# Expert outputs scattered to a row per token and rank, and two chunks' steps five tiles earlier

## The chip, the cores and the metric

The kernel runs on one core of a Trainium2 chip. The metric is the device time of one execution in microseconds. TensorE multiplies, VectorE, ScalarE and GpSimd work on rows in SBUF, SyncE (SP) issues most transfers, and GpSimd issues those whose row numbers are in a table (indirect transfers).

## The reference

The input is 2 x 1024 tokens of 128 numbers, T = 2048 rows. Two layers follow one another; each normalises its input and adds two branches to it.

```
xn = layernorm(x)
x  = x + [xn + attention(layernorm(xn))] + experts64(xn)
xn = layernorm(x)
x  = x + wkv_mix(xn) + experts8(xn)
```

Attention has 16 heads of 8 numbers, and queries and keys of unit length. `experts64` sends each token to its 3 best of 64 experts (rank 0, 1, 2). An expert takes the first 64 rows sent to it, later ones are dropped, and it computes `gelu(rows @ w1 + b1) @ w2 + b2`; a token's result is the sum of its three expert rows, each times its gate. `wkv_mix` is a recurrence over the tokens of a sequence (running maxima and two weighted sums), with a gate and an output product. `experts8` computes all 8 experts for all tokens and keeps the two best by their gates.

## The kernel before

The tokens are worked in 16 tiles of 128 rows, four tiles to a chunk, so there are four chunks of 512. Every engine has its own instruction stream, written out by hand in program order, and the engines meet only at semaphores (`wait_ge`). No scheduler moves anything: where a step stands in the code of an engine is where it runs.

The attention is the backbone. It is a loop over 128 tiles (16 groups of a chunk and four heads, 8 key tiles each): TensorE makes the scores of a tile (line 1347), ScalarE takes their exponential (line 564), TensorE multiplies by the values (line 1361). All else of the first half is put between tiles: `if n == 98: combine(0)` in VectorE's stream means that VectorE does that step when it comes to tile 98. TensorE and ScalarE have tables of the same kind.

From tile 32 to tile 79 the 64 experts run in 8 rounds of 6 tiles; a round does four pairs of experts. GpSimd gathers the rows of the pairs from `xn_rows` in DRAM with the list `IDX` (line 388), TensorE and VectorE compute, and at the end of a round VectorE writes the round's 4 x 128 output rows to `Y` (line 924, `moe_y`). SP stores `Y` to `slot_out`, a DRAM table by expert and place (lines 315 and 318). After the last round, at tile 83, GpSimd gathers each chunk's rows back, 12 indirect transfers of 128 rows for a chunk (line 397), three at a time, since each set of three waits for the one before. `YGS` holds two chunks, so chunks 2 and 3 are gathered when 0 and 1 have been used.

VectorE adds chunks 0 and 1 to `BASE` (`combine`, line 933), GpSimd chunks 2 and 3 (lines 406 and 410: a product over 1536 columns and three sums over 512). Then the second layer follows for each chunk: attention's output product, `x1_norm` (lines 945 to 954, which for chunks 2 and 3 waits for GpSimd's sums), `x1_scale` (975), transposes on TensorE (`normed`, 1473), key, value and gate products, and the recurrence: `time_mix` (1037, 1039), `time_mix_states` (1051, 1053), `time_mix_out` (1058 to 1064), `time_mix_end` (1067, 1070). GpSimd does four products of each chunk's recurrence (`mix`, 417 to 424). `finish` on TensorE (1512, 1515) closes the chunk.

Behind the attention, from about 381 us, comes the tail: 32 steps, one for each chunk and expert of `experts8` (`up2` line 1609, `down2` line 1618, `accumulate` on VectorE, line 1078), with the recurrence of chunk y put at the steps MIX_FROM[y] = 1, 11, 21 and after: VectorE does `time_mix` of chunk 1 at step 3, `time_mix_states` at step 5, `x1_norm` of chunk 2 at step 6, `time_mix_out` of chunk 1 at step 7, `x1_scale` of chunk 2 at step 8, `time_mix_end` of chunk 1 at step 9.

How the slots are found: VectorE numbers each token's place within its expert (`slots`), makes one-hot rows of places (`RANK`) and of experts times token number (`WHO`, `slot_hots`), TensorE multiplies them (`invert`, line 1440), and VectorE copies the product as `IDX` (`slot_tokens`).

Of the kernel before, what the change touches and what calls it, by code (L numbers as in the profile page):

```python
# [7 lines left out]
ALU = mybir.AluOpType  # L8
ACT = mybir.ActivationFunctionType
AX = mybir.AxisListType.X  # L10
F32 = mybir.dt.float32
# [5 lines left out]
P = 128  # L17
# [6 lines left out]
def build(nc, x_d, ln_w_d, ln_b_d, qkv_w_d, qkv_b_d, out_w_d, out_b_d, gate_w_d, gate_b_d, w1_d, b1_d, w2_d, b2_d,  # L24
# [53 lines left out]
    MIXED = (94, 109, 111, 112, 120, 125)  # L78
# [5 lines left out]
    slot_out = nc.dram_tensor("slot_out", [SLOTS, D], F32, kind="Internal").ap()  # L84

    with ExitStack() as ctx:
# [24 lines left out]
        WHO = carve(RA, 6144, 1536, F16).rearrange("p (k t e) -> p k t e", k=TOPK, e=E0)  # L111
# [65 lines left out]
        SLF = sb("slot_f", [P, TOPK, NT])  # L177
        SLG = sb("slot_gather", [P, TOPK, NT], U32)
        TOK = sb("token", [P, NT])
        IDX = sb("slot_token", [P, NPAIR], U32)  # L180
        MH = sb("mask_bf", [P, NT, E0], BF16)
# [43 lines left out]
        for i in range(4):  # L225
# [9 lines left out]
            ranked inverted slot_ready b1_in b1_ps b1_sb b2_in bt_ps bt_sb up_done h_sb gelu_done htr_ps htr_sb down_done y_sb  # L235
# [25 lines left out]
        def _(sp):  # L261
# [15 lines left out]
            sp.dma_start(WG[:], wg_d).then_inc(s["l1_in"], 16)  # L277
            sp.dma_start(MB2[:], mb2_d).then_inc(s["l1_in"], 16)
# [26 lines left out]
            for G in range(ROUNDS):  # L305
# [12 lines left out]
            sp.dma_start(slot_out[P * RING * (ROUNDS - 1):P * RING * ROUNDS].rearrange("(i p) d -> p i d", p=P), Y).then_inc(s["y_out"], 16)  # L318
# [12 lines left out]
        def _(pool):  # L331
# [4 lines left out]
                            pattern=[[-1, P]], channel_multiplier=1).then_inc(s["const_ready"], 1)  # L336
            link(g.memset(VA, 0.0))
# [8 lines left out]
                            pattern=[[1, P]], channel_multiplier=-1)  # L346
            g.iota(iota_e[:], [[1, E0]], base=0, channel_multiplier=0, allow_small_or_imprecise_dtypes=True)
# [37 lines left out]
            for m in range(NPAIR):  # L385
                if m >= RING and m % RING == 0:
                    pool.wait_ge(s["h_sb"], m)
                g.indirect_dma_start(ring_in[m % RING], None, xn_rows, bass.IndirectOffsetOnAxis(IDX[:, m:m + 1], 0),  # L388
                                     bounds_check=T - 1, oob_is_err=True).then_inc(ring_in_x[m % RING], 16)
            pool.wait_ge(s["y_out"], 16 * ROUNDS)  # L390

            def gather(c):
                for t in range(CH * c, CH * c + CH):
                    if t > CH * c:
                        pool.wait_ge(gathered[c], 16 * TOPK * (t - CH * c))
                    for k in range(TOPK):
                        g.indirect_dma_start(YGS[c % 2][:, t - CH * c, k, :], None, slot_out, bass.IndirectOffsetOnAxis(SLG[:, k, t:t + 1], 0),  # L397
                                             bounds_check=SLOTS - 1, oob_is_err=True).then_inc(gathered[c], 16)

            def combine(c):  # L400

                pool.wait_ge(gathered[c], 16 * TOPK * CH)
# [23 lines left out]
            gather(0)  # L426
            pool.wait_ge(gathered[0], 16 * TOPK * CH)
# [1244 lines left out]
```

## Time and profile before

| | us |
|---|---|
| three runs, median (lowest to highest) | 523.83 (523.05 to 525.02) |
| span of the profiled execution | 525.1 |
| the profiled execution's own time, beside its span | not given apart from the span; the highest run is 525.02 |
| TensorE matmul busy | 494.3 (94%) |
| ScalarE busy | 375.1 (71%) |
| VectorE busy | 303.1 (58%) |
| GpSimd busy | 144.1 (27%) |

The busy share of TensorE is high in every stretch, so the shares alone say little: what is to be read is where an engine waits, and for whom. In the rows, a time in brackets is the idle time of the engine just before the instruction, and behind the arrow stands what ended it. PE is TensorE (PEld its weight loads), DVE VectorE, ACT ScalarE, POOL GpSimd.

### The profile page before, as it was taken

To read this page: it belongs to the slowest core of one execution; us is meant where nothing else is said; L and a number is where in the kernel's file an instruction comes from. 1 tells how busy PE (TensorE), PEld (TensorE's weight loads), DVE (VectorE), ACT (ScalarE), POOL (GpSimd) and SP (SyncE) were. 2 spreads that over 40 slices of the span, in tenths; PEclk is the share of its full clock that TensorE was granted. 3 is DMA by queue.
4 is the path that set the end of the run, shared out by engine and by line. 5 is a ranking of instruction groups with operands and counts; after the bars stand their busy time and mean duration, and the time that the engine had idled before them with its cause. 6 is when DMAs were issued, how large, how long until landed. Compare 5 with 4: busy or idle time off the path is not lost.

```text
span 525.1 us, 11527 instructions
## 1 busy us (share of the span) xinstructions
PE 494.3 (94%) x4696; PEld 270.8 (52%) x4696; DVE 303.1 (58%) x790; ACT 375.1 (71%) x464; POOL 144.1 (27%) x133
## 2 busy tenths in 40 slices
PE   6977999999999999999998999999899999999996
PEld 5874223443455455445444232333467766767775
DVE  6799899434343343343330126367937983994895
ACT  3967988786978878978888989888535625553641
POOL 4078000303203203203000445425550755400120
PEclk8997999999999999999998999999899999999999
DMA  5200000565487877977362511100100110000000
GB/s 148 82 1 1 2 1 2 157 216 181 163 238 243 282 243 218 313 238 233 126 201 60 152 32 31 32 1 21 37 6 0 35 38 11 22 0 1 21 1 20
DMA packets 38542, 50.01 MB, mean 95 GB/s; under 512 B 3581, under 2 KB 20250, under 8 KB 38490
## 3 DMA queue, kind: packets, MB, share of 16 engines
q1 hardware_dynamic: 35524, 43.84, 25.4%
q0 software_dynamic: 2560, 5.25, 5.1%
q8 instruction: 37, 0.61, 0.5%
q10 hardware_dynamic: 406, 0.20, 0.1%
q14 instruction: 15, 0.12, 0.1%
HBM read 45.07 MB, written 4.19 MB: 94 GB/s over the span
## 4 chain that ended last, share of the span: by engine, by line
PE 50%; ACT 17%; DVE 6%; issue 5%; DVEq 0%
ACT region_b L564 11%; PE bank L1361 11%; PE scores L1609 9%; PE bank L1618 9%; PE scores L1347 5%; PE bank L1407 4%; PE bank L1395 3%; ACT xn L570 2%; PE bank L1417 2%; PE bank L1478 2%; DVE region_a L1067 2%; ACT L564 2%; ACT L570 2%; DVE base L1078 1%; PE bank L1372 1%
## 5 line engine op out<-in xcount | busy, mean ns | idle before, releaser
L564 ACT ACTIVATE region_b<-scores 128x1024 f32<-128x1024 f32 x256 | 242.4, 1045 | 51.8 <-PE scores L1347 51.6
L1361 PE MATMUL bank<-region_b 128*16 128x256 f32 x2048 | 149.0, 391 | 0.0
L1347 PE MATMUL scores<-region_b 32*128 32x512 f16 x512 | 83.0, 389 | 14.2 <-ACT region_b L564 14.0
L626 ACT ACTIVATE region_b<-scores,small_cols 128x512 f32<-128x512 f32 x64 | 43.6, 685 | 50.3 <-PE scores L1609 50.3
L388 POOL DMA_INDIRECT region_a<-xn_rows,slot_token x32 | 32.5, 1016 | 160.8 <-DVE h_rows L908 108.0
L1361 PEld LDWEIGHTS bank<-region_b 128*16 128x16 f32 x2048 | 42.0, 96 | 57.9 <-issue 42.6
L1618 PEld LDWEIGHTS bank<-region_a,region_b 128*128 128x128 f32 x512 | 62.2, 192 | 15.5 <-issue 15.3
L1347 PEld LDWEIGHTS scores<-region_b 32*128 32x128 f16 x512 | 20.8, 91 | 92.4 <-ACT region_b L564 68.9
L1618 PE MATMUL bank<-region_a,region_b 128*128 128x128 f32 x512 | 62.5, 275 | 0.0
L1609 PE MATMUL scores<-x_rows,region_a 128*128 128x512 f32 x128 | 62.3, 610 | 0.0
L1078 DVE SCALAR_TENSOR_TENSOR base<-bank,g,base 128x128 f32<-128x128 f32 x128 | 36.0, 344 | 28.0 <-PE bank L1618 27.6
L397 POOL DMA_INDIRECT xn<-slot_out,slot_gather x24 | 24.7, 1029 | 65.4 <-DMA slot_out<-slots_io 44.4
L908 DVE COPY h_rows<-bank 128x512 f32<-128x512 f32 x32 | 22.1, 692 | 24.6 <-PE bank L1395 24.6
L924 DVE TENSOR_TENSOR slots_io<-bank,region_a 128x512 f32<-128x512 f32 x8 | 5.5, 692 | 51.4 <-PE bank L1417 51.4
L1395 PE MATMUL bank<-region_a,slots_io 128*64 128x512 f32 x128 | 32.8, 609 | 0.2
L1609 PEld LDWEIGHTS scores<-x_rows,region_a 128*128 128x128 f32 x128 | 22.8, 195 | 19.5 <-issue 19.4
L1417 PE MATMUL bank<-region_a,xn 128*64 128x128 f32 x512 | 32.4, 280 | 0.5 <-issue 0.5
L1417 PEld LDWEIGHTS bank<-region_a,xn 128*64 128x64 f32 x512 | 28.4, 139 | 7.8 <-issue 6.8
L397 POOL DMA_INDIRECT y_rows<-slot_out,slot_gather x24 | 25.5, 1060 | 22.1 <-DMA y_rows<-slot_out,slot_gather 14.2
L916 DVE TENSOR_TENSOR xn<-bank,region_a 128x512 f32<-128x512 f32 x32 | 21.3, 687 | 15.6 <-PE bank L1407 15.6
L815 DVE COPY av_out<-bank 128x512 f32<-128x512 f32 x16 | 11.1, 692 | 32.8 <-PE bank L1361 30.5
L417 POOL TENSOR_TENSOR region_a<-region_a,h_rows 128x512 f32<-128x512 f32 x4 | 4.4, 1091 | 62.1 <-DVE h_rows L1037 62.1
(243 smaller groups left out, 590.6 us busy)
## 6 DMA issues: line engine op xcount, KB each, us to landing
region_a<-in_L_ffn_w SPq DMA_DIRECT2D x64, 512.0 KB, 5.3
region_a<-in_L_ffn_b SPq DMA_DIRECT2D x17, 128.0 KB, 7.2
slot_out<-slots_io SPq DMA_DIRECT2D x8, 256.0 KB, 7.7
region_a<-in_L_attn_x SPq DMA_DIRECT2D x4, 256.0 KB, 4.5
xn_rows<-xn SPq DMA_DIRECT2D x1, 1024.0 KB, 5.1
region_a<-in_L_ffn_W SPq DMA_DIRECT2D x1, 1024.0 KB, 5.9
out<-base SPq DMA_DIRECT2D x4, 256.0 KB, 2.3
region_a<-xn_rows,slot_token POOLq DMA_INDIRECT x32, 3.7
```

The costliest lines, as they stand in the source:

```text
L388: g.indirect_dma_start(ring_in[m % RING], None, xn_rows, bass.IndirectOffsetOnAxis(IDX[:, m:m + 1], 0), bounds_check=T - 1, oob_is_err=Tru ...
L397: g.indirect_dma_start(YGS[c % 2][:, t - CH * c, k, :], None, slot_out, bass.IndirectOffsetOnAxis(SLG[:, k, t:t + 1], 0), bounds_check=SLO ...
L564: a.activation(PR[:, n % PBUF, 2 * h:2 * h + 2, :], S[:, 2 * h:2 * h + 2, :], ACT.Exp, scale=SCALE).then_inc(s["exp_done"], 1)
L626: a.activation(HS[:, e % 2, k], ps[2 * (e % 2) + k][:], ACT.Relu, bias=COL[:, HC1 * e + k:HC1 * e + k + 1]).then_inc(s["relu_done"], 1)
L908: v.tensor_copy(HB[:, i], ps[5 + i % 2][:]).then_inc(s["h_sb"], 1)
L1078: last = v.scalar_tensor_tensor(y, ps[4 + 3 * (e % 2)][:, D * t:D * t + D], G8[:, c, t, e:e + 1], y, ALU.mult, ALU.add)
L1347: last = mm(S[:, j], KT[head, hg, keys], QT[head, hg, BLK * c:BLK * c + BLK], start=True, stop=True)
L1361: last = mm(AV[32 * j:32 * j + VW, cols], VA[:, tile, HG * (g % NHG) + j, :], PR[:, st % PBUF, j, cols], start=(st == 0 and half == 0), st ...
L1395: last = mm(ps[5 + i % 2][CAP * e:CAP * e + CAP, :], BT[:, P * i + CAP * e:P * i + CAP * e + CAP], ring_w1[i][:, e, :], start=True, stop=True)
L1417: last = mm(ps[7][CAP * e:CAP * e + CAP, D * i:D * i + D], HTS[:, i, P * c + CAP * e:P * c + CAP * e + CAP], ring_w2[i][:, e, c, :], start ...
L1609: mm(ps[2 * (e % 2) + k][:], MW1[:, e, P * k:P * k + P], XN2T[:, c, :], start=True, stop=True).then_inc(s["up2"], 1)
L1618: last = mm(ps[4 + 3 * (e % 2)][:, D * t:D * t + D], HS[:, e % 2, k, P * t:P * t + P], MW2[:, e, k, :], start=(k == 0), stop=(k == HC1 - 1))
```

## The change

The output table in DRAM becomes `token_out`: a row for each token and rank, in the order in which a chunk is loaded, and 128 spare rows. It is filled with zeros once from SP, near the start. The slot list gets a second half: beside the token of a slot, TensorE's product now also gives its rank plus one (`WHO` has two parts, the product 64 columns in place of 32), and VectorE works out `ROW = 3 * token + rank`, or a spare row for an empty slot. In each round GpSimd scatters the four 128-row blocks of `Y` with that list, one after another, each waiting for the one before. The 48 gathers are gone: SP loads a chunk with one plain transfer of 768 KB.

In the tables of VectorE, TensorE and ScalarE the steps of chunks 0 and 1 that stand at tile 87 or later (before: 92 or later) are moved up by five tiles; `normed(1)` and `normed_cols(1)`, which had stood behind the attention, come to tiles 124 and 125. MIX_FROM is as it was.

```diff
-    MIXED = (94, 109, 111, 112, 120, 125)
+    MIXED = (89, 104, 106, 107, 115, 120)
@@ SP
+            sp.wait_ge(s["zero_ready"], 1)
+            sp.dma_start(token_out[0:TOPK * T].rearrange("(p a r) d -> p a (r d)", p=P, r=CH),
+                         OH[:, NC - 1].rearrange("p t g w -> p (t g w)").unsqueeze(1).to_broadcast([P, TOPK * T // (P * CH), BLK])
+                         ).then_inc(s["zeroed"], 16)
             sp.dma_start(MB2[:], mb2_d).then_inc(s["l1_in"], 16)
...
-                    sp.dma_start(slot_out[P * RING * (G - 1):P * RING * G].rearrange("(i p) d -> p i d", p=P), Y).then_inc(s["y_out"], 16)
...
+            def load_rows(c):
+                rows = token_out[TOPK * BLK * c:TOPK * BLK * (c + 1)].rearrange("(t p k) d -> p t (k d)", p=P, k=TOPK)
+                sp.dma_start(YGS[c % 2].rearrange("p t k d -> p t (k d)"), rows).then_inc(gathered[c], 16)
+            sp.wait_ge(s["y_out"], 16 * RING * ROUNDS)
+            for c in range(EARLY):
+                load_rows(c)
...
+            for c in range(EARLY, NC):
+                sp.wait_ge(s["first_combined"], c - 1)
+                load_rows(c)
@@ GpSimd
+            def rows_out(G):
+                pool.wait_ge(s["y_sb"], G + 1)
+                for i in range(RING):
+                    m = RING * G + i
+                    if m:
+                        pool.wait_ge(s["y_out"], 16 * m)
+                    g.indirect_dma_start(token_out, bass.IndirectOffsetOnAxis(ROW[:, m:m + 1], 0), Y[:, i, :], None,
+                                         bounds_check=TOPK * T + P - 1, oob_is_err=True).then_inc(s["y_out"], 16)
+            rows_in(0)
+            rows_in(1)
+            pool.wait_ge(s["zeroed"], 16)
+            for G in range(2, ROUNDS):
+                rows_in(G)
+                rows_out(G - 2)
+            rows_out(ROUNDS - 2)
+            rows_out(ROUNDS - 1)
...
-            gather(0)
-            pool.wait_ge(gathered[0], 16 * TOPK * CH)
-            gather(1)
             mix(0)
-            pool.wait_ge(s["first_combined"], 1)
-            gather(2)
+            mix(1)
             combine(2)
-            mix(1)
-            pool.wait_ge(s["first_combined"], 2)
-            gather(3)
             combine(3)
             mix(2)
             mix(3)
@@ VectorE
-                    v.tensor_tensor(WHO[:, k], EQ[:, k], TOK[:].unsqueeze(2).to_broadcast([P, NT, E0]), ALU.mult)
+                    v.tensor_tensor(WHO[:, k, :, 0, :], EQ[:, k], TOK[:].unsqueeze(2).to_broadcast([P, NT, E0]), ALU.mult)
+                    v.tensor_scalar(WHO[:, k, :, 1, :], EQ[:, k], float(k + 1), None, ALU.mult)
...
-                    dve.wait_ge(s["y_out"], 16 * G)
+                    dve.wait_ge(s["y_out"], 16 * RING * G)
...
-                if n == 98:
+                if n == 93:
                     combine(0)
...
-                if n == 121:
+                if n == 116:
                     combine(1)
@@ TensorE
-                if n == 125:
+                if n == 120:
                     finish(0)
+                if n == 124:
+                    normed(1)
```

GpSimd's stream before, from the gathers of the last round (line 388) to the mixing of chunk 1: the gathers of chunk 2 and its combine (406, 410) stand between the mixing of chunk 0 (417 to 424) and that of chunk 1.

```order
L388 DMA region_a<-xn_rows,slot_token 128x128 [waits h_sb]
L388 DMA region_a<-xn_rows,slot_token 128x128 x3
...
L417 TENSOR_TENSOR region_a<-region_a,h_rows 128x512 [waits d_ready]
L419 TENSOR_TENSOR region_a<-h_rows,region_a 128x512 [waits d_ready]
L422 TENSOR_TENSOR region_a<-region_a 128x512 [waits vx_sb,d_exp]
L424 TENSOR_TENSOR region_a<-region_a 128x512 [waits d_exp]
L397 DMA xn<-slot_out,slot_gather 128x128 [waits first_combined]
...
L406 TENSOR_TENSOR xn<-xn,gates 128x1536 [waits gathered2]
L410 TENSOR_TENSOR base<-base,xn 128x512 [waits combined] x3
L417 TENSOR_TENSOR region_a<-region_a,h_rows 128x512 [waits rw_ready,d_ready]
```

GpSimd's stream of the changed kernel, a round with its scatters (line 417 there), and then the mixing of chunk 1 (446 to 453) and the two combines (435, 439).

```order
L407 DMA region_a<-xn_rows,slot_token 128x128 [waits h_sb]
L407 DMA region_a<-xn_rows,slot_token 128x128 x3
L417 DMA token_out<-slots_io,slot_row 6272x128 [waits y_out,y_sb]
L417 DMA token_out<-slots_io,slot_row 6272x128 [waits y_out] x3
...
L446 TENSOR_TENSOR region_a<-region_a,h_rows 128x512 [waits rw_ready,d_ready]
L448 TENSOR_TENSOR region_a<-h_rows,region_a 128x512 [waits d_ready]
L451 TENSOR_TENSOR region_a<-region_a 128x512 [waits vx_sb,d_exp]
L453 TENSOR_TENSOR region_a<-region_a 128x512 [waits d_exp]
L435 TENSOR_TENSOR xn<-xn,gates 128x1536 [waits gathered2]
L439 TENSOR_TENSOR base<-base,xn 128x512 [waits combined] x3
L435 TENSOR_TENSOR y_rows<-y_rows,gates 128x1536 [waits gathered3]
L439 TENSOR_TENSOR base<-base,y_rows 128x512 [waits combined] x3
```

The combine of chunk 2 has gone from ahead of the mixing of chunk 1 to behind it, that of chunk 3 follows at once, and each round's gathers are followed by four scatters in a chain.

TensorE's stream of the changed kernel at the end of the attention: the finish of chunk 0 (1536, 1539) at tile 120, and the transposes of chunk 1 (1497) at tile 124, between score matmuls (1371) and value matmuls (1385).

```order
L1536 MATMUL bank<-w_cols,region_a 128x128 x4
L1539 MATMUL bank<-mb,xn 128x128 x4
L1371 MATMUL scores<-region_b 128x512 x4
L1385 MATMUL bank<-region_b 16x256 x8
L1396 MATMUL bank<-ident,av_out 128x128 x4
...
L1497 MATMUL bank<-ident,x_rows 128x128 x4
L1371 MATMUL scores<-region_b 128x512 x2
L1385 MATMUL bank<-region_b 16x256 x4
```

Before, the finish stood at tile 125, behind the transposes of tile 121 (there line 1372, here 1396), and the transposes of chunk 1 behind the first step of the tail.

## Rows read from the trace of the kernel before

**Rows 1.** Busy by stretch: us; PE, PEld, DVE, ACT, POOL; clock, DMA share, GB/s.
```profile
285.00:366.00 81.00, 76.37 (x826) 25.27 (x818) 34.16 (x104) 73.03 (x82) 34.03 (x32) 1.00 0.19 52
...
378.00:380.00 2.00, 2.00 (x24) 0.95 (x20) 1.86 (x9) 0.00 (x0) 1.57 (x2) 0.50 0.22 51
```
**Rows 2.** Timeline (start, us, engine, line, operation), TensorE, the finish of chunk 0.
```profile
374.39 1.16 PE L1512 MATMUL bank<-w_cols,region_a 128*128 128x128 f32 x8 [0.98 <-DVE region_a L1070]
```
**Rows 3.** Timeline, VectorE, the tail.
```profile
412.04 1.25 DVE L1053 TENSOR_TENSOR_SCAN h_rows<-region_a,h_rows 128x512 f32<-128x512 f32 x1
...
414.84 0.69 DVE L945 TENSOR_TENSOR base<-base,bank 128x512 f32<-128x512 f32 x1
...
418.28 0.69 DVE L1058 TENSOR_TENSOR region_a<-region_a,h_rows 128x512 f32<-128x512 f32 x1
```
**Rows 4.** Timeline, TensorE, the tail: chunk 2's transposes and chunk 1's finish.
```profile
424.20 0.66 PE L1473 MATMUL bank<-ident,x_rows 128*128 128x128 f32 x4
...
429.42 1.16 PE L1512 MATMUL bank<-w_cols,region_a 128*128 128x128 f32 x8 [1.05 <-DVE region_a L1070]
```
**Rows 5.** Timeline, GpSimd, chunk 2's combine and the end of chunk 1's mixing.
```profile
382.14 2.75 POOL L406 TENSOR_TENSOR xn<-xn,gates 128x1536 f32<-128x1536 f32 x1 [1.66 <-DMA xn<-slot_out,slot_gather]
384.97 3.97 POOL L410 TENSOR_TENSOR base<-base,xn 128x512 f32<-128x512 f32 x3
...
409.77 1.26 POOL L424 TENSOR_TENSOR region_a<-region_a 128x512 f32<-128x512 f32 x1
411.19 1.78 POOL L397 DMA_INDIRECT y_rows<-slot_out,slot_gather  x1 [0.15 <-issue]
```
**Rows 6.** Timeline, VectorE and GpSimd at the same time.
```profile
351.26 1.86 DVE L1045 SCALAR_TENSOR_TENSOR region_a<-region_a,small_cols 128x512 f32<-128x512 f32 x1
...
352.54 1.72 POOL L422 TENSOR_TENSOR region_a<-region_a 128x512 f32<-128x512 f32 x1
...
357.10 1.26 POOL L424 TENSOR_TENSOR region_a<-region_a 128x512 f32<-128x512 f32 x1 [2.85 <-ACT region_a L618]
357.22 1.69 DVE L1058 TENSOR_TENSOR region_a<-region_a,h_rows 128x512 f32<-128x512 f32 x1
...
387.00 1.13 DVE L1078 SCALAR_TENSOR_TENSOR base<-bank,g,base 128x128 f32<-128x128 f32 x4 [2.81 <-PE bank L1618]
```
**Rows 7.** Timeline of a round, and landing times of the gathers of `xn_rows`.
```profile
160.54 1.01 POOL L388 DMA_INDIRECT region_a<-xn_rows,slot_token  x1 [14.84 <-DVE h_rows L908]
...
166.21 0.69 DVE L924 TENSOR_TENSOR slots_io<-bank,region_a 128x512 f32<-128x512 f32 x1 [6.45 <-PE bank L1417]
...
172.54 0.68 DVE L895 COPY slots_io<-bank 128x512 f32<-128x512 f32 x1
...
180.33 1.01 POOL L388 DMA_INDIRECT region_a<-xn_rows,slot_token  x1 [14.83 <-DVE h_rows L908]
...
DMA to landing us min/median/max: 2.8/3.8/7.5
```
**Rows 8.** Transfers: the page's GB/s in 40 slices, an issue, and timeline rows.
```profile
GB/s 148 82 1 1 2 1 2 157 216 181 163 238 243 282 243 218 313 238 233 126 201 60 152 32 31 32 1 21 37 6 0 35 38 11 22 0 1 21 1 20
...
xn_rows<-xn SPq DMA_DIRECT2D x1, 1024.0 KB, 5.1
...
284.22 0.69 DVE L924 TENSOR_TENSOR slots_io<-bank,region_a 128x512 f32<-128x512 f32 x1 [9.59 <-PE bank L1417]
...
302.09 1.00 POOL L397 DMA_INDIRECT xn<-slot_out,slot_gather  x1 [2.30 <-DMA xn<-slot_out,slot_gather]
...
314.08 2.05 DVE L933 SCALAR_TENSOR_TENSOR base<-xn,gates,base 128x128 f32<-128x128 f32 x7 [0.41 <-DMA xn<-slot_out,slot_gather]
```
**Rows 9.** Timeline, the slot lists: a cast, TensorE's product, VectorE's idle time.
```profile
77.36 0.69 DVE L800 CAST h_rows<-region_a 128x1024 f16<-128x1024 f32 x1
...
93.18 1.70 PE L1440 MATMUL bank<-region_a 128*64 128x32 f16 x96
...
98.45 0.69 DVE L815 COPY av_out<-bank 128x512 f32<-128x512 f32 x1 [3.33 <-PE bank L1361]
```

More of the change, by code:

```diff
@@ L384, in _, with rows_in @@
             pool.wait_ge(s["late_split"], 2 * (NC - EARLY))
[L385 to L398, printed above, removed]
+            def rows_in(G):
+                if G:
+                    pool.wait_ge(s["h_sb"], RING * G)
+                for i in range(RING):
+                    m = RING * G + i
+                    g.indirect_dma_start(ring_in[i], None, xn_rows, bass.IndirectOffsetOnAxis(IDX[:, m:m + 1], 0),
+                                         bounds_check=T - 1, oob_is_err=True).then_inc(ring_in_x[i], 16)
+            def rows_out(G):
+                pool.wait_ge(s["y_sb"], G + 1)
+                for i in range(RING):
+                    m = RING * G + i
+                    if m:
[10 more added lines that the diff above has]
+            rows_out(ROUNDS - 1)
             def combine(c):
-                pool.wait_ge(gathered[c], 16 * TOPK * CH)
+                pool.wait_ge(gathered[c], 16)
                 chunk = slice(CH * c, CH * c + CH)
@@ L926, in combine @@
             def combine(c):
-                dve.wait_ge(gathered[c], 16 * TOPK * CH)
+                dve.wait_ge(gathered[c], 16)
                 if c:
@@ L1153, in _ @@
                     time_mix(0)
-                if n == 112:
+                if n == 107:
                     values_in(0)
-                if n == 113:
+                if n == 108:
                     gates(0)
-                if n == 114:
+                if n == 109:
                     time_mix_first(0)
-                if n == 116:
+                if n == 111:
                     gates_cols(0)
                     time_mix_states(0)
-                if n == 117:
-                    attention_rows(1)
-                if n == 118:
-                    time_mix_out(0)
-                if n == 121:
-                    combine(1)
+                if n == 112:
+                    attention_rows(1)
+                if n == 113:
+                    time_mix_out(0)
+                if n == 116:
+                    combine(1)
+                if n == 117:
+                    time_mix_end(0)
+                if n == 119:
+                    x1_norm(1)
+                if n == 120:
+                    x1_scale(1)
                 if n == 122:
-                    time_mix_end(0)
-                if n == 124:
-                    x1_norm(1)
+                    mixed(0)
                 if n == 125:
-                    x1_scale(1)
-                if n == 127:
-                    mixed(0)
+                    normed_cols(1)
             evacuate(NG - 1)
@@ L1439, in invert @@
                         for odd in range(2):
-                            last = mm(ps[6][CAP * odd:CAP * odd + CAP, 0:NPAIR], RANK[:, k, t, :], WHO[:, k, t, odd:E0:2],
+                            last = mm(ps[6][CAP * odd:CAP * odd + CAP, 0:2 * NPAIR], RANK[:, k, t, :], WHO[:, k, t, :, odd:E0:2],
                                       start=(k == 0 and t == 0), stop=(k == TOPK - 1 and t == NT - 1), skip_group_check=True)
@@ L1580, in _ @@
                     slots_in(0)
-                if n == 92:
+                if n == 87:
                     attention_cols(0)
-                if n == 94:
+                if n == 89:
                     attention_out(0)
+                if n == 101:
+                    normed(0)
+                if n == 104:
+                    keys_logits(0)
                 if n == 106:
-                    normed(0)
-                if n == 109:
-                    keys_logits(0)
+                    values_in(0)
+                if n == 107:
+                    receptance(0)
+                if n == 110:
+                    gates_out(0)
                 if n == 111:
-                    values_in(0)
-                if n == 112:
-                    receptance(0)
+                    attention_cols(1)
                 if n == 115:
-                    gates_out(0)
-                if n == 116:
-                    attention_cols(1)
+                    attention_out(1)
                 if n == 120:
-                    attention_out(1)
-                if n == 125:
                     finish(0)
+                if n == 124:
+                    normed(1)
             for half in range(2):
```

54 lines of the change are left out of this document (27 added, 27 removed).

## The prediction

> **What bounds the kernel now.** I read in this order: the busy shares by stretch, the waits of each engine, and then the timeline wherever the change puts an instruction. From 285 to 366 us, the 38 or so attention tiles behind the last expert round, TensorE is busy for 76.4 of 81.0 us and ScalarE for 73.0 [rows 1]: two engines that hand each other one tile at a time, so that a step put in there costs nearly its whole TensorE time wherever it stands. What is not work there is 4.6 us of TensorE idle time. From 381 us on TensorE alone paces the second layer (32 steps of the second expert layer), and it stops only where VectorE's chain for the next chunk is late: at 429.42 it had stood idle for 1.05 us, for VectorE's product of line 1070 [rows 4]. So in that tail VectorE's chain for chunk 2 has no slack, and what lengthens it lengthens the program.
>
> **The change part by part.** The sum is made against the profiled execution, whose span is 525.1 us; the median of the runs shown is 523.83, so 1.3 is taken off at the end.
>
> *Expert rounds.* GpSimd's queue gets, behind the four gathers of each round, four scatters that wait for one another. A gather is issued every 1.31 us, so four take 5.25. A scatter isn't in this trace; the nearest rows are gathers of the same 128 rows of 512 B: 2.30 us idle behind a 1.01 us issue without other traffic [rows 8], and 2.8, 3.8 and 7.5 (least, median, most) from issue to landing beside the weight loads [rows 7]. With 0.3 for the next issue, one scatter takes s = 3.3 to 7.8 us; I take 4.1, by the median, because the weights load in both. A round is 19.8 us (160.54 to 180.33), in which GpSimd now idles for 14.8 [rows 7]. Four gathers, three full scatters and the issue of the fourth are 5.25 + 3 x 4.1 + 1.3 = 18.9: they fit, barely, up to s = 4.4. The bank that they empty is written at 166.21 + 0.69, so the next gathers would be issued at 166.9 + 12.3 + 1.3 = 180.5 instead of 180.33; their rows are used some 4 us after they land (gathers from 160.54, last landing near 167.5, columns copied at 172.54 [rows 7]). I cost it at nothing; the cover is those 4 us. VectorE's wait for the buffer (four full scatters, 16.4) ends within the round too. SP loses eight stores, nothing waits on that.
>
> The Trainium skill, SBUF — State Buffer (SBUF: two separate sides), warns that a DMA issued by GpSimd stalls while VectorE runs an operation that holds the port pair shared by the two; it names about 620 ns growing to 3100. By it the scatters would cost what the rival of late scatters costs. The rows of this trace bear it out only beside operations with two SBUF inputs: the issue at 411.19 took 1.78 us beside VectorE's scan that ended at 412.12, against 1.01 otherwise [rows 5, 8]; in the rounds VectorE reads PSUM.
>
> *Slots (70 to 100 us).* Three scalar products of 1024 halfwords are added and three operations of 48 elements taken away. The nearest row, a cast of the same size, is 0.69 [rows 9]; a two-input product of half the elements is 0.69 too [rows 3], so 1.4 each is the upper end. I take 3 x 0.69 = 2.1 (upper end 4.2), and five more operations of some 0.2 before the slot list: 1.1. VectorE then idles for 3.33 us before 98.45 [rows 9], which hides the 3.2 (of the upper end, 2 us would show). The 96 matmuls of the list take 1.70 us with 32 columns [rows 9] and get 64: between 0 and 1.7 more, and I take 0.5. The zeros (3.1 MB) leave from SP behind the 1 MB that landed in 5.1 us [rows 8], so they take some 16 us; the queues move 2 GB/s or less from 26 to 92 us [rows 8], and what stands behind the zeros is 4 KB that TensorE awaits ahead of the tile loop, past 45 us (tile 10 is at 77 [rows 9]): nothing.
>
> *Chunks 0 and 1 five tiles early.* The last bank is written at 284.9 [rows 8]; four scatters without other traffic at 3.35 give 298.3, and 768 KB at the pace of that 1 MB store 4 to 5 us more: 303. VectorE began tile 98's combine at 314.08, with 0.41 us of waiting for data [rows 8], and five tiles of some 2.1 us before that is 303.5. It fits; a lateness of up to 2 us is hidden by the tiles that ScalarE still has in hand. What is gained lies at the end of attention. Now the finish of chunk 0 stands at tile 125, held by 0.98 us [rows 2], and after that idle time the granted clock was 0.50 from 378 to 380 [rows 1], the lower of the two levels (1.2 GHz), under the last value matmuls. At tile 120 VectorE's combine no longer stands behind the division of tile 121, and no gap is left: -1.0 for the gap and -1.0 for two microseconds at half clock. The four transposes for chunk 1 (0.66 by the like group at 424.20 [rows 4]) leave the tail and enter tile 124: nothing net. Together -2.0.
>
> *Tail.* The two combines on GpSimd now stand behind the mixing of chunk 1, whose last product ended at 409.77 + 1.26 = 411.03 [rows 5]. In the kernel before they had been done at 388.94, while TensorE was on step 1. One combine is 2.75 + 3.97 us [rows 5], 6.8 with its waits, so it can't end before 418.0; but VectorE's norm of chunk 2 starts at 414.84 [rows 3] and needs it. That alone is 3.2 us. Then the engines get in each other's way: VectorE's product at line 1058 took 1.69 us while GpSimd's product of 357.10 to 358.36 ran [rows 6], against 0.69 at 418.28 [rows 3], and GpSimd's at 352.54 took 1.72 beside VectorE's of 351.26 to 353.12, against 1.26 [rows 6, 5]. In each case the second one ended as if it had begun when the first was over. VectorE's accumulation of a PSUM bank beside GpSimd's sum was not held (1.13 for four, at 387.00 [rows 6]). So: scan to 412.12; GpSimd's 2.7 us product to 414.85; VectorE's second scan, issued at 412.04, to 415.95; three sums to 417.15, 418.4 and 419.65; the norm starts at 419.75, 4.9 late. Next comes chunk 3's combine on GpSimd from 419.75: product to 422.5, then sums that alternate with VectorE's five products of lines 1058 to 1064, which end at 429.1 instead of 423.15 + 3.3 = 426.5: 2.6 more. The rest of the chain (two accumulations, the scaling, a reciprocal and a product) has at most one input from SBUF or stands behind the sums, and TensorE, which waited 0.3 us for chunk 2's rows at 424.20 and 1.05 for the finish, is held by all of it: +7.5. Nothing gives it back, as each later step is TensorE's own.
>
> Sum: 0 + 0.5 - 2.0 + 7.5 = +6.0, so 531.1 against the 525.1 of the profiled execution and 529.8 against the median.
>
> **The rivals.**
>
> *No interference, only the queue.* GpSimd and VectorE run side by side and only the 3.2 us to 418.0 count: 0.5 - 2.0 + 3.2 = +1.7, 525.5. For it: the accumulations were not held. Against: the two pairs above.
>
> *Late scatters.* With s = 5 a round needs 5.25 + 15 + 1.3 = 21.6 against 19.8. The first gathers are 2.9 us late, which the 4 us hide, and each of the next four rounds adds 1.75: 2.9 + 7.0 - 4 = +5.9 on top, 535.7. For it: one group in the rows has 7.5 us. Against: the median, 3.8. The Trainium skill, DMA: Bandwidth & Descriptors (Anatomy of one DMA — SWDGE (gpsimd) path), gives 2.0 us and 436 GB/s, about 2.2 for 64 KB, as an estimate from that page; by it s would be under 3.5 and this rival empty, but the loaded rows are above it.
>
> *The other side: attention closes its gaps.* The place is tiles 84 to 127. If the steps land five tiles earlier where ScalarE is ahead, the 4.6 us of TensorE idle time [rows 1] go too. Then -2.0 - 4.6 + 0.5 = -6.1 stands against the tail, and it decides from a tail cost under 6.1: with 3.2 it gives 525.1 - 2.9 = 522.2, or 520.9 by the median. Against it: the order of work and its amount are kept, only the place changes.
>
> *The early steps come too early.* If the last four scatters and the two loads end at 306 or later, the change doesn't do what it says: VectorE's combine waits at tile 93 past the 2 us of cover, the copy of tile 96's bank stands behind it, and TensorE with it: with s = 4.8 the data come at 309, 5 us late, +3, 532.8.
>
> **How the numbers follow.** What a measurement of this kernel tells from no change is some 0.5%, that is 521.2 to 526.4. Forecast 0.52 (own range 526.5 to 533: a second half-speed spell or less interference); only the queue 0.17; late scatters 0.13; closed gaps 0.11; too early 0.07. Closed gaps alone are faster: 0.11. Same: 0.16 of the queue and 0.02 of the forecast at its low end: 0.18. Slower is the rest, 0.71. The range 523.0 to 536.0 takes in the queue, the forecast, most of the early steps and half of the late scatters, 0.82, and leaves out the closed gaps and the upper end of s.
>
> **What would show it.** In the tail, VectorE's norm of chunk 2 (line 969 of the changed kernel) waits for GpSimd's sum (line 439) for 3 to 5 us, the five products after it take well over 0.69 each, and TensorE idles for 5 us or more before the transposes of chunk 2. At the end of attention the finish of chunk 0 has no idle time ahead of it. In the rounds the scatters start every 4 us or so and the gathers still follow VectorE's copies. I am wrong if GpSimd's sums end before VectorE asks for them, if the pairs run side by side at their usual lengths, or if the rounds grow past 19.8 us.

## The result and the profile after

The changed kernel takes 549.24 us (median), the kernel before 523.44 in the same runs: ratio 1.0458, 95% interval 1.0383 to 1.0533. (A ratio here compares fast executions only, one of the changed kernel's four being a slow one of 555.34, and is not the quotient of the two medians.) It is slower, as forecast, but by some 26 us and not by 6; 549 lies outside the range of 523 to 536.

The traced execution took 549.19 us with a span of 547.4, 22.3 more than the span before. In every run the time is some 1.8 us above the span, so the traced execution before, with its span of 525.1, was some 3.4 us slower than its kernel's median; that is why the spans differ by 22.3 and the medians by 25.8.

Four events cut both spans into the same work: VectorE's first and last write of `Y` (line 948, before 924), TensorE's first matmul of the tail (1635, before 1609) and VectorE's last accumulation (1102, before 1078; the start of its last group of four).

| stretch, us | before | after | difference | forecast |
|---|---|---|---|---|
| start to the first write | 146.42 | 146.33 | -0.1 | +0.5 |
| first to last write: seven rounds | 137.80 | 157.50 | +19.7 | 0 |
| last write to the tail: the rest of attention | 96.74 | 93.70 | -3.0 | -2.0 |
| tail, to the last accumulation | 140.18 | 145.97 | +5.8 | +7.5 |

Three of the four terms lie within 2 us of the forecast. The one that was costed at nothing is nearly the whole loss. The busy table over that second stretch, first of the kernel before, then of the changed one (columns: stretch, length, then busy time and count of PE, PEld, DVE, ACT, POOL, then granted clock, DMA share, GB/s):

```profile
146.42:284.22 137.80, 133.67 (x1546) 70.92 (x1546) 50.99 (x100) 113.96 (x126) 20.22 (x20) 0.99 0.69 221
```
```profile
146.33:303.83 157.50, 139.60 (x1546) 72.40 (x1546) 51.19 (x100) 113.97 (x126) 48.46 (x48) 0.95 0.64 193
```

The same 1546 matmuls. TensorE's idle time grew from 4.1 to 17.9 us (+13.8), and its busy time by 5.9, while the granted clock fell from 0.99 to 0.95: TensorE stops more often, and part of its work runs at a lower clock: the granted clock was 0.66 from 171 to 176 us and 0.57 from 198 to 206 and from 243 to 251, where stops of 2.62, 3.25 and 6.10 us ended (at 171.39, 200.39 and 244.87), and 1.00 between these stretches. The transfers move less per microsecond than before (193 against 221 GB/s).

Who waits, by the table of waits from 140 to 310 us (engine and line, for whom; total us, times, longest):

```profile
POOL token_out L417 <- DMA token_out<-slots_io,slot_row: 86.0, 21, 7.0
...
DVE slots_io L948 <- DMA token_out<-slots_io,slot_row: 22.6, 2, 12.3
...
PE bank L1396 <- DVE slots_io L948: 6.1, 1, 6.1
PE bank L1407 <- DMA region_a<-xn_rows,slot_token: 4.8, 2, 3.2
...
PE bank L1431 <- DVE xn L940: 2.6, 1, 2.6
```

GpSimd waits for its own scatters, and twice VectorE waits for the chain too. The three rows of TensorE, none of which the kernel before has, are 13.5 of its 13.8 us of new idle time: 8.7 end behind VectorE, which had stood with its write of `Y`, and 4.8 with the landing of gathered rows. GpSimd's timeline, one round and the last one, which answers to [rows 7]:

```profile
172.53 1.03 POOL L417 DMA_INDIRECT token_out<-slots_io,slot_row  x1 [0.30 <-issue]
178.26 1.01 POOL L417 DMA_INDIRECT token_out<-slots_io,slot_row  x1 [4.70 <-DMA token_out<-slots_io,slot_row]
181.31 0.98 POOL L417 DMA_INDIRECT token_out<-slots_io,slot_row  x1 [2.05 <-DMA token_out<-slots_io,slot_row]
187.24 0.98 POOL L417 DMA_INDIRECT token_out<-slots_io,slot_row  x1 [4.95 <-DMA token_out<-slots_io,slot_row]
188.53 1.06 POOL L407 DMA_INDIRECT region_a<-xn_rows,slot_token  x1 [0.30 <-issue]
...
305.30 0.98 POOL L417 DMA_INDIRECT token_out<-slots_io,slot_row  x1 [4.00 <-DVE slots_io L948]
308.32 0.98 POOL L417 DMA_INDIRECT token_out<-slots_io,slot_row  x1 [2.04 <-DMA token_out<-slots_io,slot_row]
```

Read the starts. When nothing else is moving (after 305) a scatter follows the one before by 3.02 us: 0.98 of issue, 2.04 of waiting. In the first six rounds the 18 distances within a round run from 3.02 to 8.08 and average 5.3. The issue itself is never longer than 1.04. So the gathers at 188.53 come 8.2 us later than the one at 180.33 in [rows 7], directly behind the last scatter. What the chain does to VectorE and TensorE, one round earlier:

```profile
169.95 0.69 DVE L948 TENSOR_TENSOR slots_io<-bank,region_a 128x512 f32<-128x512 f32 x1 [10.26 <-DMA token_out<-slots_io,slot_row]
170.56 0.68 DVE L940 TENSOR_TENSOR xn<-bank,region_a 128x512 f32<-128x512 f32 x1
171.16 0.68 DVE L837 COPY av_out<-bank 128x512 f32<-128x512 f32 x1
```
```profile
171.39 0.92 PE L1431 MATMUL bank<-ident,h_rows 128*128 128x128 f32 x4 [2.62 <-DVE xn L940]
```

The write of `Y` stands 10.26 us at the head of VectorE's queue; the copies behind it (lines 940 and 837) are what TensorE needs.

The tail went as the prediction told it. VectorE, GpSimd and TensorE, answering to [rows 3 to 5]:

```profile
428.18 3.70 DVE L1077 TENSOR_TENSOR_SCAN h_rows<-region_a,h_rows 128x512 f32<-128x512 f32 x1
...
435.77 0.69 DVE L969 TENSOR_TENSOR base<-base,bank 128x512 f32<-128x512 f32 x1 [2.73 <-POOL base L439]
...
440.16 1.76 DVE L1083 TENSOR_TENSOR region_a<-region_a,h_rows 128x512 f32<-128x512 f32 x1
441.96 1.63 DVE L1084 TENSOR_TENSOR region_a<-region_a 128x512 f32<-128x512 f32 x1
```
```profile
425.91 1.26 POOL L453 TENSOR_TENSOR region_a<-region_a 128x512 f32<-128x512 f32 x1
427.14 3.66 POOL L435 TENSOR_TENSOR xn<-xn,gates 128x1536 f32<-128x1536 f32 x1
430.88 4.76 POOL L439 TENSOR_TENSOR base<-base,xn 128x512 f32<-128x512 f32 x3
```
```profile
439.82 2.05 PE L1644 MATMUL bank<-region_a,region_b 128*128 128x128 f32 x16 [1.39 <-ACT region_b L648]
447.49 1.12 PE L1497 MATMUL bank<-ident,x_rows 128*128 128x128 f32 x4 [5.62 <-DVE x_rows L999]
```

From the end of the mixing to the norm of chunk 2 it is 8.60 us (427.17 to 435.77), before 3.81 (411.03 to 414.84): 4.79 late, forecast 4.9. VectorE's second scan takes 3.70 in place of 1.25, beside GpSimd's product. TensorE stops for 1.39 and 5.62.

### The profile page after: what moved, and what is told of

The parts are those of the page before. It is cut to its first block, busy times and chain, and to the rows that moved or that the text cites. A ratio compares the mean times of both kernels' runs of the same rounds, so it can differ in the third digit from the quotient of the medians.

```text
span 547.4 us, 11509 instructions
## 1 busy us (share of the span) xinstructions
PE 498.3 (91%) x4696; PEld 271.5 (50%) x4696; DVE 306.6 (56%) x795; ACT 374.8 (68%) x464; POOL 129.2 (24%) x119
## 4 chain that ended last, share of the span: by engine, by line
PE 42%; DMA 11%; ACT 11%; issue 6%; DVE 5%; POOL 3%; POOLq 0%; DVEq 0%
DMA token_out<-slots_io,slot_row 10%; PE bank L1385 9%; PE scores L1635 8%; ACT region_b L586 8%; PE bank L1644 8%; PE scores L1371 5%; PE bank L1419 2%; PE bank L1502 2%; PE bank L1431 2%; PE bank L1441 1%; DMA region_a<-xn_rows,slot_token 1%; DVE base L1102 1%; ACT xn L592 1%; PE bank L1396 1%; ACT L586 1%
## 5 line engine op out<-in xcount | busy, mean ns | idle before, releaser
L1371 PE MATMUL scores<-region_b 32*128 32x512 f16 x512 | 83.7, 394 | 13.8 <-ACT region_b L586 13.5
L417 POOL DMA_INDIRECT token_out<-slots_io,slot_row x32 | 31.9, 996 | 108.3 <-DMA token_out<-slots_io,slot_row 90.1
L1431 PE MATMUL bank<-ident,h_rows 128*128 128x128 f32 x128 | 22.7, 311 | 2.6 <-DVE xn L940 2.6
```

The source lines that it names most:

```text
L417: g.indirect_dma_start(token_out, bass.IndirectOffsetOnAxis(ROW[:, m:m + 1], 0), Y[:, i, :], None, bounds_check=TOPK * T + P - 1, oob_is_e ...
L1371: last = mm(S[:, j], KT[head, hg, keys], QT[head, hg, BLK * c:BLK * c + BLK], start=True, stop=True)
L1431: last = tr(ps[5 + i % 2][:, P * c:P * c + P], cols[:, c, :], ident[:])
```

## The experiments

The stretches of the table above in each run, with the time and the ratio to the kernel before:

| run | rounds | attention | tail | time | ratio (95%) |
|---|---|---|---|---|---|
| free scatters | 136.69 | 93.71 | 145.96 | 530.11 | 1.0119 (1.0050 to 1.0187) |
| combines ahead of mixing, chain kept | 159.18 | 100.22 | 138.10 | 549.63 | 1.0505 (1.0433 to 1.0576) |
| both | 136.65 | 100.22 | 138.10 | 526.51 | 1.0054 (1.0023 to 1.0085) |
| thin loads, chain kept | 138.12 | 93.71 | 145.43 | 530.92 | 1.0126 (1.0054 to 1.0199) |
| free, combines in the quiet stretch | 137.80 | 94.35 | 139.81 | 522.21 | 0.9941 (0.9912 to 0.9969) |
| free, old tiles | 137.67 | 95.30 | 148.80 | 533.03 | 1.0158 (1.0110 to 1.0207) |
| two chains | 136.65 | 93.70 | 146.04 | 529.30 | 1.0104 (1.0056 to 1.0152) |
| chain kept, two buffers for `Y` | 165.57 | 93.69 | 145.36 | 556.38 | 1.0586 (1.0527 to 1.0646) |
| free, only chunk 2 in the quiet stretch | 136.66 | 93.70 | 140.38 | 523.76 | 0.9993 (0.9964 to 1.0022) |

The kernel before took 524.64 us (median) beside the first four runs, 525.29 beside the next four and 524.98 beside the last. The time is a median, the stretches are those of one traced execution; the stretch ahead of the rounds, left out here, ran from 145.13 to 148.53 us.

### Free scatters

```diff
-                    if m:
-                        pool.wait_ge(s["y_out"], 16 * m)
...
-        SPARE = sb("spare_row", [P, 1])
+        SPARE = sb("spare_row", [P, NPAIR])
...
```

> The scatters of a round no longer wait for one another (each has spare rows of its own, so that no two write one row); all else is as in the changed kernel. Theory of the chain: what costs the 19.6 us by the last bank (303.83 against 284.22) is the time to landing of each scatter, put one behind the other on GpSimd's queue; issued every 1.3 us, four gathers and four scatters take 10.5 us of a round, the banks are written every 19.8 us again, the last at 284 to 286, and the program takes 549.2 - 19.6 = 529.6 us (528 to 531). Rival, the row writes themselves: the scatters are slow because 512-byte writes share the DMA engines with the weight loads; then four at once only move the waiting to VectorE's write of the buffer, the rounds stay at 22 us or more, and the program takes 540 us or more.

530.11 us, and the last write at 284.54 (284.22 before). GpSimd issues the same 32 scatters 1.3 us apart:

```profile
169.18 1.03 POOL L415 DMA_INDIRECT token_out<-slots_io,slot_row  x1 [2.13 <-DVE slots_io L946]
170.52 1.01 POOL L415 DMA_INDIRECT token_out<-slots_io,slot_row  x1 [0.31 <-issue]
171.83 0.98 POOL L415 DMA_INDIRECT token_out<-slots_io,slot_row  x1 [0.30 <-issue]
173.12 0.98 POOL L415 DMA_INDIRECT token_out<-slots_io,slot_row  x1 [0.30 <-issue]
181.85 1.06 POOL L407 DMA_INDIRECT region_a<-xn_rows,slot_token  x1 [7.75 <-DVE h_rows L930]
```

The gathers wait for VectorE's copies again, as in [rows 7]. The bytes are the same, and so are the rows written, but for the spare ones; neither the bytes nor the number of writes costs the rounds anything: the waits between the scatters do. The rival falls. Nor do the spare rows, which the changed kernel's scatters share, explain the slow landings: with rows of their own the scatters still took 5.9 us (median) from issue to landing here, four under way, and 5.0 in the run with two chains.

### The combines ahead of the mixing of chunk 1

```diff
-            mix(1)
             combine(2)
             combine(3)
+            mix(1)
```

> The chain stays; GpSimd combines chunks 2 and 3 before it mixes chunk 1. Theory of the tail: the norm of chunk 2 no longer waits for GpSimd (4.79 us later than in the kernel before, counted from the mixing) and the five products of lines 1082 to 1088 take 0.69 each; the tail, 5.8 us longer than before by the last accumulation, loses all of it, so 549.2 - 5.8 = 543.4 us (542.5 to 544.5). Rival, the tail is longer because of the granted clock and not the queue: the combines cost the same wherever they stand, less than 2 us are won, 547 us or more.

A miss: 549.63, nothing won. The tail is 7.9 us shorter (138.10), more than expected, but the attention is 6.5 longer (100.22) and the rounds 1.7. The rival's time came true, but not its cause: the tail did get shorter. The next run, with the same edit and free scatters, shows the same two numbers and is read for both.

### Both edits

> Both edits, the free scatters and the earlier combines. If the two costs are separate (theory of the chain, theory of the tail), they add up: 549.2 - 19.6 - 5.8 = 523.8, about the kernel before, or a little less, as the attention after the rounds took 3.0 us less than before and that stays: from the kernel before, 523.4 - 3.0 = 520.4. So 520 to 524 us. Rival, the combines stand in the way of the early steps or of the mixing when the rounds no longer delay everything: 526 us or more.

526.51: 3.6 less than free scatters alone, yet above the range; the rival (526 or more) is what came. The two costs are separate (136.65 in the rounds, 138.10 in the tail), but the price of the combines has moved. VectorE's timeline in the end of attention, and GpSimd's beside it:

```profile
348.92 1.75 DVE L1081 TENSOR_TENSOR region_a<-region_a,h_rows 128x512 f32<-128x512 f32 x1
350.70 1.65 DVE L1082 TENSOR_TENSOR region_a<-region_a 128x512 f32<-128x512 f32 x1
...
364.82 2.00 DVE L980 TENSOR_SCALAR var_n<-mean_var 128x4 f32<-128x4 f32 x1
366.85 0.17 DVE L981 TENSOR_SCALAR rstd_n<-var_n 128x4 uint32<-128x4 uint32 x1
367.05 1.12 DVE L982 TENSOR_SCALAR rstd_n<-rstd_n 128x4 int32<-128x4 int32 x1
```
```profile
348.52 4.95 POOL L437 TENSOR_TENSOR base<-base,xn 128x512 f32<-128x512 f32 x3
364.04 2.75 POOL L433 TENSOR_TENSOR y_rows<-y_rows,gates 128x1536 f32<-128x1536 f32 x1 [10.56 <-DMA y_rows<-token_out]
```

An operation on four numbers per partition, 0.16 us with free scatters alone, takes 2.00 here: it begins 0.78 us after GpSimd's product and ends at 366.82, when the product does (366.79). The whole inverse root takes 7.1 us (364.82 to 371.89) in place of 2.3. The products of chunk 0 and the norm of chunk 1 are now what GpSimd collides with.

The Trainium skill, SBUF — State Buffer (SBUF: two separate sides), says that a VectorE operation in a two-port mode, or with two inputs from SBUF where the GpSimd operation reads SBUF, and a GpSimd operation share a port pair: the one that starts first keeps it for its whole length, and the other is blocked, not slowed. This trace agrees: both ends lie within 0.03 us. The mode of a VectorE operation stands in no profile, so that the small one ran in a two-port mode is not shown.

### Thin loads

```diff
-                sp.dma_start(ring_w1[i], w1_d[2 * m:2 * m + 2].rearrange("e p h -> p e h")).then_inc(ring_in_a[i], 16)
+                cols = slice(0, H0 if m < RING else 64)
+                sp.dma_start(ring_w1[i][:, :, cols], w1_d[2 * m:2 * m + 2].rearrange("e p h -> p e h")[:, :, cols]).then_inc(ring_in_a[i], 16)
...
```

> The chain stays, but from the second round on the loads of the expert weights move an eighth of the up weights' columns and of the down weights' columns (the later experts compute with what is left of the first round's). Theory: a scatter takes 3.03 us by itself and 5.3 on average in the first six rounds because the weights load beside it; with thin loads it takes 3.0 to 3.5, a round's queue is 5.25 + 3 x 3.3 + 1.3 = 16.5 us, under 19.8, the last bank is written at 284 to 287, and the program takes 530 us (528 to 533). Rival, the chain is slow whatever loads beside it (the writes wait on the gathers' rows or on their own queue): over 540 us with scatters of 5 us.

530.92. The chain is there, the loads move an eighth, and the rounds are whole. GpSimd, one round:

```profile
169.34 1.03 POOL L419 DMA_INDIRECT token_out<-slots_io,slot_row  x1 [2.13 <-DVE slots_io L950]
172.54 1.00 POOL L419 DMA_INDIRECT token_out<-slots_io,slot_row  x1 [2.17 <-DMA token_out<-slots_io,slot_row]
175.71 0.98 POOL L419 DMA_INDIRECT token_out<-slots_io,slot_row  x1 [2.16 <-DMA token_out<-slots_io,slot_row]
```

The 18 distances average 3.34 us (3.02 to 4.76) in place of 5.3. So the chain costs only what the weight loads make of each landing. With the first run: chain with an eighth of the loads, 0.3 us in the rounds; loads without chain, nothing; both, 19.7 us.

### The combines in VectorE's quiet stretch

```diff
-            mix(1)
+            pool.wait_ge(s["fin_sb"], 1)
             combine(2)
             combine(3)
+            mix(1)
```

> Free scatters, and both of GpSimd's combines stand between the first and the second mixing, but only after VectorE has added chunk 0's mixing to the residual (a wait for fin_sb), where VectorE sits idle for 4.42 and 4.06 us of the next 15 (369 to 384 in the run with free scatters alone). Theory of contention: in the run with both edits the combines stretched VectorE's products of chunk 0 (L1080 to L1084 from 2.7 to 6.0 us) and its inverse root (L980 to L986 from 2.3 to 7.0), and the attention took 6.5 us more; beside an idle VectorE they cost nothing, so both the attention (93.7 us) and the tail (140.2) are short: the last accumulation comes at 284.4 + 93.7 + 140.2 = 518.3 and the program takes 521.8 us (520 to 523.5). Rival, the combines cost the same some 4 to 6 us wherever they are put, because VectorE's work in the stretch is too dense: 526 us or more, as with both edits.

522.21, as expected, and the fastest of all: 0.6% under the kernel before. GpSimd's sums run at their own pace:

```profile
370.42 2.75 POOL L433 TENSOR_TENSOR xn<-xn,gates 128x1536 f32<-128x1536 f32 x1 [21.21 <-DVE base L1109]
373.25 3.98 POOL L437 TENSOR_TENSOR base<-base,xn 128x512 f32<-128x512 f32 x3
377.19 2.75 POOL L433 TENSOR_TENSOR y_rows<-y_rows,gates 128x1536 f32<-128x1536 f32 x1
380.02 3.96 POOL L437 TENSOR_TENSOR base<-base,y_rows 128x512 f32<-128x512 f32 x3
```

All four lengths are within 0.01 us of those of [rows 5], and the tail is 139.81. The same work costs next to nothing here: its price was its place, not its amount.

### The old tiles

The numbers of the tables of VectorE, TensorE and ScalarE go back by five tiles, on free scatters.

> Free scatters as in the first run, but the steps of chunks 0 and 1 stand at the tiles of the kernel before (undoing the five tiles). Theory of the gap: the attention after the rounds took 93.7 us instead of 96.7 because the finish of chunk 0 no longer holds TensorE at tile 125; with the old tiles it takes 96.7 again, and the program 530.1 + 3.0 = 533 us (532 to 534.5). Rival, the gathers' absence: 48 gathers less on GpSimd's queue and on the ports gave the 3 us, and the tiles nothing: 530 us (529 to 531).

533.03, the time that was expected, but the trace supports only half of the reason. The intervals of its ratio and of that of free scatters alone overlap (1.0110 to 1.0207, 1.0050 to 1.0187). The attention takes 95.30, not 96.7: 1.6 of the 3.0 come back, and of these 0.98 is the idle time ahead of chunk 0's finish, as in [rows 2]:

```profile
373.21 1.16 PE L1534 MATMUL bank<-w_cols,region_a 128*128 128x128 f32 x8 [0.98 <-DVE region_a L1092]
```

Another 2.8 us are in the tail (148.80 against 145.96): chunk 1's transposes are back in it, and from 480 to 484 us the clock was 0.73, where free scatters alone have 1.00. Why the lower level came there is open. The rounds are 1.0 longer, and the stretch ahead of them 2.7 shorter (145.13 against 147.85): the clock of its first 70 us was 1.00 here and 0.90 with free scatters alone, so the two traces differ by more than the tiles. Of the 3.0, 1.4 do not come back. In the trace before, the clock was 0.60 from 376 to 380 us, which by an estimate (four microseconds of work at 0.60 in place of 1.00) is worth 1.6; here it was 1.00.

### Two chains

```diff
+                    done = s["y_odd" if m % 2 else "y_out"]
+                    if m > 1:
+                        pool.wait_ge(done, 16 * (m // 2))
...
```

The spare rows are those of the free scatters.

> Two chains in place of one: the even and the odd scatters of a round wait only for their own kind (two semaphores), so two are under way at a time. Theory of the chain: the queue of a round is 5.25 for the gathers, one landing of 5 to 8 us and three issues of 1.3, 14 to 17 us, under the 19.8 of a round; the rounds are back at 19.8, and the program takes 530 us (529 to 532), the same as with no waits. Rival, the number of row writes in flight counts (each slows the other, and the weight loads): a time between, 534 to 542 us.

529.30, no different from no waits at all. Two under way at a time are enough, since a round's queue then ends within the round.

### Two buffers for the outputs

```diff
+        Ys = (Y, y_odd[:, 0:RING * P].rearrange("p (i d) -> p i d", d=D))
...
-                    dve.wait_ge(s["y_out"], 16 * RING * G)
+                    dve.wait_ge(s["y_out"], 16 * RING * (G - 1))
...
```

> The chain stays, but VectorE writes the outputs of two rounds to two buffers in turn, so that its write waits only for the scatters of the round before the last. It tells which of the chain's two victims carries the loss. Theory of the queue: GpSimd itself is full (four gathers 5.25, three scatters of 5.3 on average, one issue 1.3: 22.5 us and more against 19.8), and its late gathers hold the rounds; the second buffer wins little, the last bank is written at 298 to 304 and the program takes 543 to 549 us. Rival, the held buffer: the 22.6 us that VectorE waited (10.26 and 12.31) are what passed on to TensorE; without them the rounds drift apart and the program takes 530 to 538 us.

556.38: outside both ranges, 7 us slower than the changed kernel. So the held buffer was not the source of the loss (that rival asked for 530 to 538), though 8.7 us of TensorE's idle time had ended behind it; without it the late gathers strike TensorE directly. Waits from 140 to 310 us, and the timeline of TensorE:

```profile
PE bank L1408 <- DMA region_a<-xn_rows,slot_token: 21.4, 3, 7.5
```
```profile
181.34 1.09 PE L1408 MATMUL bank<-ident,region_a 128*128 128x128 f32 x4 [7.51 <-DMA region_a<-xn_rows,slot_token]
```

TensorE's wait for gathered rows was 4.8 us in the changed kernel. The theory of the queue had the right engine, but it forecast a small gain where there was a loss: I take it that VectorE's wait had kept the rounds in step with the gathers; this is argued, not shown.

### Only chunk 2 in the quiet stretch

Against the run with both combines in the quiet stretch:

```diff
             pool.wait_ge(s["fin_sb"], 1)
             combine(2)
-            combine(3)
             mix(1)
+            combine(3)
```

> As in the run before with both combines in VectorE's quiet stretch, but only chunk 2's combine stays there; chunk 3's goes back behind the second mixing, where no instruction waits for it before the next chunk. So the wait of the norm of chunk 2 is gone and only the sharing of the ports is left. Theory of contention: GpSimd's product of 2.75 us stands beside VectorE's second scan (1.25 us there, 3.70 in the changed kernel), which ends 2.5 us later, and the sums are over before the products; the tail takes 139.8 + 2.5 = 142.3 us, the program 522.2 + 2.5 = 524.7 us (523.7 to 526). Rival, only the queue (the wait for the sums is the whole price of the tail, 6.3 us): no loss, 522 us (521 to 523).

523.76, at the lower edge of the range of contention and above that of the queue. The intervals of this run and of the quiet one overlap a little, so the trace decides: no instruction waits for GpSimd's sums, and still VectorE's second scan is long and TensorE stops.

```profile
408.90 3.71 DVE L1076 TENSOR_TENSOR_SCAN h_rows<-region_a,h_rows 128x512 f32<-128x512 f32 x1
```
```profile
423.40 0.66 PE L1496 MATMUL bank<-ident,x_rows 128*128 128x128 f32 x4 [2.47 <-DVE x_rows L998]
...
428.55 1.16 PE L1535 MATMUL bank<-w_cols,region_a 128*128 128x128 f32 x8 [0.99 <-DVE region_a L1093]
```

That is 3.46 us of stops against 1.05 in the quiet run, 2.4 more, as expected (2.5). The tails differ by 0.57 only: TensorE's busy time in them is 1.7 us less here (135.65 against 137.35), as from 428 to 436 us the clock was 0.73 and 0.84 in the quiet run's trace and 1.00 in this one. The quiet run's traced execution was also the slowest of its twelve (524.88), so the 1.55 us between the two medians is a fairer measure, below the 2.5 that was expected.

## Why the prediction was wrong, and where it was right

*Expert rounds: the step that failed.* "I cost it at nothing" rested on "one scatter takes s = 3.3 to 7.8 us; I take 4.1, by the median, because the weights load in both". It measured 5.3 on average, from 3.02 to 8.08. It was not the choice of a median over a mean: the scatters' own median is 5.4. The rows were those of other transfers, gathers, at another place in the round. In the trace before, the queues moved 191 to 210 GB/s in the 7 to 8 us behind the first gather of a round and 275 to 313 in the 12 us until the next, where the scatters came to stand; whether that, or writing in place of reading, made the difference, no run tells. The fit held "barely, up to s = 4.4", and the term of nothing became 19.7 us; thin loads show the other side of that line: at 3.34 the rounds are whole.

*The rival of late scatters* named the mechanism and was given 0.13 and 5.9 us at s = 5. Its own working with 5.3 gives: a round of 5.25 + 15.9 + 1.3 = 22.45, first gathers 3.8 late, four more rounds of 2.65, less 4 of cover, 10.4 us. Measured were 19.7. Of the rest, 5.9 is TensorE's longer busy time at the lower clock, which the working had no term for. The last 3.4 or so fit a path that the working had ruled out: "VectorE's wait for the buffer ends within the round" failed with the same s, VectorE's write stood for 10.26 and 12.3 us, and of TensorE's new idle time 8.7 us ended behind it and only 4.8 with the late rows. How the two paths share the rounds beyond that is not shown.

By the Trainium skill, DMA: Bandwidth & Descriptors (Anatomy of one DMA — SWDGE (gpsimd) path), 64 KB take 2.0 us plus the bytes at 436 GB/s, about 2.2 as an estimate, and the semaphore fires only when the last byte has landed. The trace has 3.02 from issue to issue without other traffic, 2.04 of it waiting behind the issue, and 5.3 beside the loads; the page's figure has no term for load, and the measurement decides.

*GpSimd's issue beside VectorE.* That VectorE would hold the issues was given as a way to late scatters; in the rounds an issue took 0.98 to 1.06, so it did not.

*Without the chain's waits* the program took 530.11 us beside 524.64 for the kernel before: +5.5, where the other three terms were forecast at +6.0. That closeness is in part luck: the traces give these terms as -0.1 - 3.0 + 5.8 = +2.7, against a traced execution before that was itself some 3.4 above its median.

*Slots.* -0.1 instead of +0.5; but that stretch differs by up to 3.4 us between the traces (145.13 to 148.53), so half a microsecond can't be read from it.

*Five tiles earlier.* It fits, though with less room than forecast: VectorE waited 4.66 us for the load before chunk 0's combine, beyond the 2 us of cover, and still TensorE was busy for 17.72 of the 18 us to 322. The gap ahead of the finish is gone, and no stretch of 4 us at the end of attention has a clock below 1.00 ([rows 1]: 0.50 from 378 to 380). The old tiles bring back the gap but not the half clock, so "two microseconds at half clock" is not shown to belong to the tiles.

*Tail.* Right in mechanism and near in size. Queue: 4.79 for 4.9. Contention: the five products took 5.5 us instead of 3.3, 2.1 more for 2.6. TensorE started on chunk 2's rows 6.7 us late (447.49 against 424.20, less the 16.57 by which the tail began later); the 1.05 that it used to wait for the finish had gone into that, which the +7.5 counted again: 5.7, and 5.8 measured. The rival of the queue alone is refuted by these lengths, and by the run with only chunk 2 in the quiet stretch, where TensorE stops for 2.47 us though nothing waits for GpSimd's sums.

*Closed gaps* did not come: with free scatters the attention is 93.71, all of it in the 3.0 already told.

## What to carry to other kernels

A chain of transfers, each waiting for the landing of the one before, must be priced by the mean landing under the traffic of its own stretch; rows of other transfers in another stretch mislead (here 4.1 for 5.3). Where they write different rows, give the leftovers rows of their own and drop the waits. An engine's late work can cost twice where the matmul engine stops for it: the stop, and a lower clock after it (13.8 and 5.9 us in the rounds here; after the stop of 2.47 us in the last run the clock stayed at 1.00). Before moving GpSimd's elementwise work, look for a stretch in which VectorE is idle, since elsewhere the same work only moves its price.

## What the hardware showed

VectorE's smallest operations suffer most, for their length, beside GpSimd's: 128 x 4 numbers went from 0.16 to 2.00 us beside a product of 128 x 1536, and a scan of 1.25 us to 3.70, while four accumulations from PSUM stay near 1.13 beside GpSimd's sums [rows 6]. Four scatters in flight beside the loads cost the rounds nothing, but one after another they cost 5.3 us each, and 3.3 with loads of an eighth.
